# Gated cross-attention and ternary feed-forward: the hidden block turned by transposing transfers instead of by TensorE

## What is computed

```python
x = x + jnp.tanh(g_xattn[0]) * _L0_xattn_ref(_layernorm(x, axis=-1), ctx_1024, ctx_1024, mask, Wq, Wk, Wv, Wo)
x = x + jnp.tanh(g_ffn[0]) * _L0_ffn_ref(_layernorm(x, axis=-1), w_gate, w_up, w_down)

def _act_quant(x):
    scale = 127.0 / jnp.clip(jnp.max(jnp.abs(x), axis=-1, keepdims=True), 1e-05)
    xq = jnp.clip(jnp.round(x * scale), -128.0, 127.0) / scale
...
def _L0_ffn_ref(x, w_gate, w_up, w_down):
    gate = jax.nn.silu(_bitlinear(x, w_gate))
    up = _bitlinear(x, w_up)
    return _bitlinear(gate * up, w_down)
```

## Time and profile before

| | us |
|---|---|
| median of 3 runs (1491.0 to 1491.93) | 1491.89 |
| the profiled execution | 1492.94 |
| its span, first to last instruction | 1491.1 |
| PE busy in the span | 1392.6 (93%) |
| DVE busy | 1063.0 (71%) |
| ACT busy | 974.9 (65%) |
| POOL busy | 706.1 (47%) |

### The profile page before, as it was taken

How to read it: one execution, slowest core, us unless ns; L and a number is a source line. 1 busy time by engine, 2 the same in 40 slices (tenths; PEclk the granted TensorE clock), 3 DMA queues, 4 the chain that set the end, 5 groups by cost and what they waited for, 6 DMA issues and landing times.

```text
span 1491.1 us, 29273 instructions
## 1 busy us (share of the span) xinstructions
PE 1392.6 (93%) x9088; PEld 742.1 (50%) x9408; DVE 1063.0 (71%) x2513; ACT 974.9 (65%) x1404; POOL 706.1 (47%) x1187
## 2 busy tenths in 40 slices
PE   6446999999999999999999999999999999998987
PEld 3123454545545454555545455554545455554543
DVE  6966778676777868677777867677786867776664
ACT  2664775848486684848567584948658484855855
POOL 2042544636354464636454463635446463643652
PEclk9767999999999999999999999999999999999999
DMA  8661303122140402113040212213040311202100
GB/s 297 195 163 57 92 16 95 40 85 51 49 102 14 119 14 91 49 56 79 20 131 14 87 46 82 51 41 101 20 123 15 92 49 56 77 21 64 37 15 29
DMA packets 86885, 105.86 MB, mean 71 GB/s; under 512 B 24366, under 2 KB 58030, under 8 KB 85320
## 3 DMA queue, kind: packets, MB, share of 16 engines
q1 hardware_dynamic: 86856, 105.51, 24.2%
HBM read 61.64 MB, written 35.46 MB: 65 GB/s over the span
## 4 chain that ended last, share of the span: by engine, by line
PE 73%; DVE 11%; ACT 6%; issue 6%; POOL 1%; SPq 1%; DMA 1%; ACTq 0%; DVEq 0%; POOLq 0%
PE bank L1153 22%; PE bank L1175 15%; PE bank L994 7%; PE bank L995 7%; PE bank L996 7%; PE bank L1072 4%; PE bank L1091 2%; PE bank L1164 2%; ACT region L689 2%; PE bank L1103 2%; PE bank L1047 2%; PE bank L1094 1%; ACT up L677 1%; DVE region L942 1%; PE bank L1092 1%
## 5 line engine op out<-in xcount | busy, mean ns | idle before, releaser
L553 POOL TENSOR_TENSOR region<-region,up 128x512 f32<-128x512 f32 x256 | 331.6, 1298 | 353.3 <-DVE region L942 218.0
L1153 PE MATMUL bank<-tern_gate,region 128*128 128x512 fp8e4 x1024 | 264.2, 380 | 5.5 <-DVE region L942 4.7
L1153 PE MATMUL bank<-tern_up,region 128*128 128x512 fp8e4 x1024 | 263.7, 380 | 0.0
L1175 PE MATMUL bank<-tern_down,region 128*128 128x512 fp8e4 x1024 | 231.8, 379 | 11.4 <-ACT region L689 11.4
L544 POOL TENSOR_TENSOR work<-work 124x512 f16<-124x512 f32 x160 | 185.9, 1175 | 100.8 <-ACT work L644 93.3
L942 DVE SCALAR_TENSOR_TENSOR region<-region,bank 128x512 f32<-128x512 f32 x256 | 171.7, 680 | 59.6 <-ACT region L669 59.0
L677 ACT ACTIVATE up<-bank 128x512 f32<-128x512 f32 x256 | 155.1, 606 | 79.7 <-PE bank L1153 79.3
L669 ACT ACTIVATE region<-bank,fs 128x512 f32<-128x512 f32 x256 | 177.0, 692 | 32.2 <-PE bank L1153 30.9
L948 DVE TENSOR_REDUCE hmx<-region 128x1 f32<-128x512 f32 x256 | 167.7, 676 | 5.9 <-POOL region L553 5.9
L681 ACT ACTIVATE region<-region,fs 128x2048 f32<-128x2048 f32 x64 | 128.4, 2006 | 57.1 <-DVE fs L959 57.0
L653 ACT ACTIVATE region<-region,fs 128x512 f32<-128x512 f32 x64 | 46.2, 722 | 180.5 <-DVE fs L935 180.5
(11 more groups left out here) (147 smaller groups left out, 2557.5 us busy)
## 6 DMA issues: line engine op xcount, KB each, us to landing
q_stack<-q_rows SPq DMA_DIRECT2D x96, 256.0 KB, 4.6
xbig<-in_x SPq DMA_DIRECT2D x16, 1024.0 KB, 5.6
q_rows<-q SPq DMA_DIRECT2D x64, 256.0 KB, 2.1
out_y<-o SPq DMA_DIRECT2D x64, 256.0 KB, 2.0
q_stack<-mT SPq DMA_DIRECT2D x32, 256.0 KB, 3.9
region<-in_wgT SPq DMA_DIRECT2D x4, 1024.0 KB, 14.2
region<-in_wuT SPq DMA_DIRECT2D x4, 1024.0 KB, 5.3
region<-in_wdT SPq DMA_DIRECT2D x4, 1024.0 KB, 4.8
```

The source lines that it names most:

```text
L553: nc.gpsimd.tensor_tensor(ht, ht, up[:, n % 2, :], ALU.mult).then_inc(hmul_ready, 1)
L1153: ins = T.matmul(pb[2 * (n % 2) + w][:, :], xqT[:, k, tok], tern[w][:, k * FF + n * GT:k * FF + (n + 1) * GT], start=(k == 0), stop=(k == ...
L1175: ins = T.matmul(pb[2][:, :], hT[:, t % 2, k, :], tern[2][:, k * GT:(k + 1) * GT], start=(k == 0), stop=(k == FK - 1))
```

## The change

The step `hT` on PE and its two copies on ACT are gone. In their place ACT subtracts 1.5 * 2^23 from the 2048 scaled words and writes them as bf16 to a new tile `hb` (`hb`, L699 of the changed kernel), and SP issues one transposing DMA for each token tile, from `hb` (128x2048 bf16, 512 KB) to `hT` (`tH`, L458 of the changed kernel). `down` waits for that transfer. `hb` has one buffer, so the `hb` of the next tile waits for the transfer too; `h` is free once `hb` has been read, and banks 0 and 1 no longer take part in the turning. The order tables of all engines and all three programs are replaced.

```diff
+        hb = sb("hb", [P, FF], bf16)
...
+            def h_transposed(f, t, _):
+                sp.wait_ge(hb_ready, f * TT + (t + 1))
+                if f * TT + t >= 2:
+                    sp.wait_ge(down_mm, f * TT + (t - 1))
+                sp.dma_start_transpose(hT[:, t % 2, :, :], hb[:, :]).then_inc(hT_in[t % 2], 16)
...
-                        act.wait_ge(hT_mm, f * (TT * 2) + (t - 1) * 2)
+                        act.wait_ge(hb_ready, f * TT + (t - 1))
...
-            def h_transposed(f, t, _):
-                for half in range(2):
-                    act.wait_ge(hT_mm, f * (TT * 2) + (2 * t + half + 1))
-                    if half == 0 and t >= 2:
-                        act.wait_ge(down_mm, f * TT + (t - 1))
-                    nc.scalar.activation(hT[:, t % 2, 8 * half:8 * half + 8, :],
-                                         pb[half][:, :].bitcast(i16).rearrange("p (c n) -> p c n", c=8),
-                                         ACT.Copy).then_inc(hT_ready, 1)
+            def h_integers(f, t, _):
+                act.wait_ge(hq_ready, f * TT + (t + 1))
+                act.wait_ge(hT_in[(t + 1) % 2], f * 32 + 16 * ((t + 1) // 2) + 16)
+                nc.scalar.activation(hb[:, :], h[:, t % 2, :], ACT.Copy, bias=-MAGIC).then_inc(hb_ready, 1)
...
-            def h_transpose(f, t, _):
-                pe.wait_ge(hq_ready, f * TT + (t + 1))
-                for half in range(2):
-                    if t < TT - 1:
-                        pe.wait_ge((silu_ready, up_ready)[half], f * (TT * FN) + ((t + 1) * FN + 3))
-                    for k in range(8):
-                        lo = (8 * half + k) * P
-                        ins = T.transpose(pb[half][:, k * P // 2:(k + 1) * P // 2].bitcast(bf16), low_words(h[:, t % 2, lo:lo + P]), ident16[:, :])
-                    ins.then_inc(hT_mm, 1)
-
             def down(f, t, _):
-                pe.wait_ge(hT_ready, f * (TT * 2) + (2 * t + 2))
+                pe.wait_ge(hT_in[t % 2], f * 32 + 16 * (t // 2 + 1) + 16)
```

More of the change, by code:

```diff
@@ L68 @@
+    F:xq20 F:xq30 A:s30 A:s31 F:gu11 A:mT00 F:gu12 F:gu13 A:sc00 A:sc01 A:sc02 A:sc03 F:gu20 A:sc04 A:sc10
+    F:down00 A:sc11 A:pv00 F:gu21 A:pv01 F:gu22 A:pv02 A:sc12 A:sc13 A:pv03 F:gu23 A:aT00 A:sc14 F:gu30 A:aT10
+    F:down10 A:pv10 N:xT00 N:xT10 A:pv11 F:gu31 A:pv12 F:gu32 A:pv13 N:xT20 N:xT30 A:aT20 F:gu33 A:aT30 F:down20
+    A:wo00 A:wo10 A:wo20 A:wo30 F:down30
 """
 SCALAR_ORDER = """
-    A:q00 A:q10 F:xq00 A:q20 A:q30 F:xq10 F:gu00 F:up00 F:gu01 F:up01 F:up02 F:gu02 F:gu03 F:up03 F:xq20 F:xq30
@@ L75 @@
+    F:up10 F:gu10 F:gu11 F:up11 A:mT00 F:hq00 F:hb00 F:up12 F:gu12 A:sc00 F:gu13 A:sc01 A:sc02 F:gu20 F:up13
+    A:sc03 A:sc04 A:sc10 F:up20 F:hq10 F:hb10 F:gu21 F:up21 A:sc11 F:gu22 F:up22 A:sc12 F:gu23 A:aT00 F:up23
+    A:sc13 F:up30 A:aT10 A:sc14 F:gu30 F:hq20 F:hb20 F:gu31 F:up31 N:xT00 F:gu32 N:xT10 F:up32 A:aT20 F:gu33
+    F:up33 N:xT20 A:aT30 N:xT30 F:hq30 F:hb30 A:zq00 A:zq10 A:zq20 A:zq30
 """
 VECTOR_ORDER = """
-    A:q00 A:q10 N:ln00 A:q20 A:q30 A:s00 F:gu00 A:s01 F:gu01 A:s10 A:s11 F:hm00 A:s20 A:s21 F:gu02 F:gu03 F:hm01
@@ L133 @@
+    A:aT10 F:down10 A:pv10 F:gu31 A:pv11 F:gu32 A:pv12 F:gu33 A:pv13 A:aT20 A:aT30 F:down20 A:wo00 A:wo10 A:wo20
+    F:down30 G:xq00 A:wo30 G:xq10 G:gu00 G:gu01 G:gu02 G:gu03 G:gu10 G:xq20 G:xq30 G:gu11 G:gu12 G:gu13 G:gu20
+    G:down00 G:gu21 G:gu22 G:gu23 G:gu30 G:down10 G:gu31 G:gu32 G:gu33 G:down20 G:down30
 """
 SCALAR_LAST = """
-    A:q00 F:xq00 A:q10 F:xq10 A:q20 A:q30 F:up00 F:gu00 F:gu01 F:up01 F:up02 F:gu02 F:gu03 F:up03 F:xq20 F:xq30
-    F:gu10 F:up10 F:gu11 F:up11 A:mT00 F:gu12 F:hq00 F:up12 F:gu13 F:hT00 F:up13 A:sc00 A:sc01 A:sc02 A:sc03
```

134 lines of the change are left out of this document (66 added, 68 removed).

## The result

The changed kernel takes 1498.89 us (median of 5 runs, 1498.63 to 1501.38) against 1491.93 for the kernel before: a ratio of 1.0050, with an interval of 1.0035 to 1.0064. It is half a per cent slower, where I had forecast 2.7% faster. The profiled execution took 1501.38 us, its span 1499.6.

The account below looks back on a forecast made before the run. PE was taken as the bound. From 1492.9 us profiled, 35 came off for fourteen groups, 2.5 for the last group's attention half and 3 for the set-up: 1452, as a median 1451, range 1434 to 1500.

Parts of the forecast that it names:

- The sum: A looping group: 85.24 less 3.56 and 0.65, plus 1.7 of new waits, 82.7 us; in total 1452 us for the profiled execution.
- PE as the bound, and what is taken off it: PE busy 84.11 of 85.24 us a group; removing the transposes takes 0.89 us a tile, 3.6 a group, off its queue.
- the price of 282 us: A skill page's about 275 ns per 128x128 transpose, applied to 1024 transposes; the prediction set it aside for the trace's row.
- L: Time of one transposing DMA from issue to landing, taken as 5 us, range 2.7 to 9.5; hidden in the loop.
- the estimate by bytes: The transfer priced from the skill's bandwidths plus a store's fixed part: 2.3 to 3.0 us.
- The room walked for `down00`: Time between `hb00` being ready on ACT and `down00` starting on PE, for the first tile's transfer: 5.5 us.
- rival 1: Slow transfer holds PE before `down`: 1455 to 1488 us (L 5.5 to 7.5, chance 0.13), up to 1608 (above 7.5, 0.20).
- ACT: right in sum: `hb` costs ACT about what the two copies did, 1.90 to 2.01 us against 1.81 a tile; busy time within 10 of 975.
- The walk: New orders on DVE, PE and ACT, timed from `mh00`'s end on DVE to `down00`: 1.7 us of new PE waiting a group.
- a wash: Last group's feed-forward: some 4 us won from first tiles' blocks and waits, some 4 more paid at the very end.
- The set-up's 3 us of gain: New set-up tables send `mT` without value loads ahead of it: 3 us gained, between -5 and +8.
- rival 2: New orders lose more than 1.7 us, with DVE unbroken and `x` behind the last store: another 1.5 a group, 1473; chance 0.12.

Follow-up runs that it names:

- ln_one: `ln_moved` with `hq`, ACT's rounding to integers, also left out, so ACT writes `hb` straight from the scaled product: 1467.46 us, 0.9828 of the kernel before.
- no_transfer: `x_first` with 60 of the 64 transposing transfers left out and their semaphore raised by SP instead: 1484.05 us, 0.9934 of the kernel before.
- twice: `x_first` with every transposing transfer issued twice, first into a tile nobody reads, `hb` and `down` waiting for both: 1492.82 us, 1.0003 of the kernel before.
- ln_moved: `x_first` with the next group's layer norm moved out of the head of DVE's loop to later places: 1478.48 us, 0.9904 of the kernel before.
- x_first: The changed kernel with SP's loop loading `x` ahead of the value loads for parts 2 and 3: 1488.02 us, 0.9968 of the kernel before.
- combined: `ln_moved` with the set-up's order tables of the kernel before on all five engines: 1478.35 us, 0.9905 of the kernel before.

## Why the prediction was wrong

The sum missed by 49 us (1452 against the 1501.4 of the profiled execution). By the table above that is 23 us for a normal period of 84.5 us in place of 82.7, thirteen times, 11.4 at the changes of batch, 4.9 at the start, 7 in the last period (2.0 longer, where the fourteenth group and the attention half of the last had 5 of gain) and 4.7 at the end, less 2 for the two long early periods before. The sign turns on the changes of batch: without their 11.4 us the kernel is faster.

**PE as the bound, and what is taken off it: nearly right.** PE's busy time fell by 3.0 us a group and not 3.56. Part of the 0.5 may lie in the view: by line, the bounds read 3.3 us a group and not 2.9, the scores 6.3 and not 6.0, and both now stand ahead of new waits, where the end of a piece is no longer hidden under its successor. That is argued and not tested. The sign that PE's busy time would fall by 68 us was wrong by the prediction's own rows, since 64 times 0.89 is 57; it fell by 38, and that also excludes the price of 282 us which the prediction set beside its own. `ln_one`, with waits of 0.2 to 0.3 beside the one at `gu12`, comes to 83.24.

**The transfer: right, and milder than forecast.** L was 3.7 us against the 5 taken and the range of 2.7 to 9.5, and above the 2.3 to 3.0 of the estimate by bytes. The room walked for `down00` was 5.5; in the trace it is 6.1 (from 603.3 to 609.39). `no_transfer` shows that rival 1 costs nothing in the loop, `twice` that a landing 5.7 us behind the first issue is still in time in a normal group and late at a change of batch. The rival to which I gave the most was the wrong one.

**ACT: right in sum.** `hb` took 1.91 us, ACT's total moved by 1.0. What I missed is what the prediction itself had noted, that `hb` must follow `hq` at once: with `mT`, `hq`, `hb` and the exponentials in one piece ACT has no gap left behind `mT`, and becomes the next limit.

**The walk: right up to the two xn.** It put `gu12` at 1.65 us, `sc03` at 7.0 and `down00` at 10.3 behind the packing's end at 598.2; the rows say 1.7, 7.9 and 11.2. The term that failed is the price of the two `xn`, "for an undisturbed `xn` I estimate 0.5". Undisturbed that is right (0.54), but these stand beside POOL's product and took 1.96 us together; my own row had 1.12 for one. That is 0.57 at `gu13`. The waits of this stretch were 2.1 us and not 1.7.

**The step that failed in the loop.** I walked one stretch of the group and began it where the packing ends, so DVE's queue ahead of it was outside of the walk: the statistics at the head, with the `q` behind them, and so 0.43 and 0.47 us at the bounds and at `mT`, where before only 0.16 stood, at an `xq`. The sum took a period of 82.7; it was 84.5. By its parts: 0.5 from PE's work, 0.4 in the walked stretch, 0.7 ahead of it, and the 0.24 at `down20`, which I hadn't walked either. `ln_moved` shows that this part was real and could be had back.

**The change of batch: missed.** I had the move in front of me ("the load of `x`, now behind the last store") and priced it only for a normal group. In three groups ten loads of values stand in between (5.2 us of SP's queue, 401.24 to 406.42). It cost 11.4 us and `x_first` gives them back. Nothing in a normal period shows it.

**The ends.** For the last tile I had 4 us more at the end and as much gained elsewhere in that part: "a wash". From the start of the last `hq` to the last `down` it is 2.9 us more (7.7 and not 4.8), and 1.8 come on top by the clock, a term that I put at nothing. That is the whole 4.7, so the gain of 4 did not come: the blocks went, but PE's waits in that part sum to 18.4 us and not 10.5. The largest new one besides the last is 2.35 us at a `gu` for a silu, and twice (1.01 us each) `gu` waits for the output of a `down` that stands ahead of it in the new order. The set-up's 3 us of gain had the wrong sign: it lost about 2.

**The rivals.** What happened is rival 2, which I gave 0.12: its places were named, DVE without a break, `ln` at the head, `x` behind the store (which costs nothing in a normal group). Its loss was put at 1.5 us a group; it was 1.8 in a normal one and 3.4 to 4.2 on top in three. The time lies just inside my range, which reached to 1500, on the side to which I gave 0.22; that it lies inside is no merit of the sum, since the range was drawn for rival 1. Without the three groups it would be the 1488 of `x_first`, and a small gain.

The version to keep is `ln_moved` (`combined` measures the same): the transfer, `x` ahead of the values, the layer norm where DVE has time, 0.96% faster than the kernel before.

## What to carry to other kernels

When work leaves the bound engine, walk the whole period on the next two engines, not only around the edit. The gain ends where the next engine has no slack left, and lightening that one shows the one behind it (84.51, 83.87, 83.24 us a period, with ACT's share worth nothing alone). Small DVE steps on a critical chain, those with two inputs in SBUF above all, are best kept clear of a product on POOL. When a DMA issue is moved in a queue, list what stands ahead of it in every kind of iteration, the rare ones too. A transfer that replaces an engine's work is free in a loop with room for it (3.7 us in 6.1 here), and fully open once at the end, where PE also loses its clock.
